# A four-layer graph network on one core: moved waits, moved exponentials, one moved matmul group and one moved scatter turn

## The reference, cut to what matters

```python
edge_index = jnp.stack([src, dst])
h = jnp.maximum(_layernorm(x, axis=-1), 0.0)
x = x + _L0_gnn_ref(h, ...)     # RGCN, 3 layers, 3 relations: relu(x[src] * (edge_attr @ nn_w.T + nn_b)), mean by (relation, dst), @ W[r]
h = jnp.maximum(_layernorm(x, axis=-1), 0.0)
x = x + _L1_gnn_ref(h, ...)     # gate = sigmoid(silu(rbf @ W1 + b1) @ W2 + b2); segment sum of gate * h[src]; update MLP
h = jnp.maximum(_layernorm(x, axis=-1), 0.0)
x = x + _L2_gnn_ref(h, ...)     # relational attention, below
h = jnp.maximum(_layernorm(x, axis=-1), 0.0)
x = x + _L3_gnn_ref(h, ...)     # distance attention, normalised by source node
```

```python
h_stack = jnp.einsum('ni,rdi->rnd', x, W)                 # 8 relations
h_src = h_stack[edge_type, src].reshape(-1, N_HEADS, HEAD_DIM)
h_dst = h_stack[edge_type, dst].reshape(-1, N_HEADS, HEAD_DIM)
attn = jax.nn.leaky_relu(sum(h_src * a_src) + sum(h_dst * a_dst), negative_slope=0.2)
attn = jax.nn.softmax(attn, axis=0)                       # over all edges
out = jax.ops.segment_sum(h_src * attn, dst, num_segments=num_nodes)
```

## Time and profile before

| what | us |
| --- | --- |
| median of 3 runs | 4981.04 |
| lowest and highest | 4974.59, 4981.15 |
| the profiled execution, its own time | 4983.89 |
| its span | 4982.0 |
| busy: PE, DVE, POOL, ACT | 3979.3, 3409.0, 3202.8, 1799.4 |

### The profile page before, as it was taken

One profiled execution on the slowest core, in us unless ns is written; L12 is line 12 of the kernel. 1 busy time (PEld: TensorE's weight loads), 2 busy tenths in 40 slices (PEclk: granted clock), 3 DMA queues, 4 the chain that ended last, 5 costly groups with the idle time before them and its releaser, 6 DMA issues. The chain is left out here.

```text
span 4982.0 us, 109658 instructions
## 1 busy us (share of the span) xinstructions
PE 3979.3 (80%) x22466; PEld 3275.0 (66%) x22467; DVE 3409.0 (68%) x9196; ACT 1799.4 (36%) x5526; POOL 3202.8 (64%) x3524
## 2 busy tenths in 40 slices
PE   6799996689987889878898466785967878578886
PEld 3477775677876778767787356674856667357665
DVE  7788886567756778577786667865237777755665
ACT  0454543121123333333332100012246667357774
POOL 0255554677756777667776677765677777247775
PEclk9799998899998999989999677897968888777787
DMA  1233333855525555264550787832454445234445
GB/s 45 91 120 120 117 120 98 196 143 153 161 61 172 147 145 159 58 191 136 149 160 21 229 246 218 243 101 82 144 101 107 102 102 105 57 97 108 108 109 99
DMA packets 633882, 637.83 MB, mean 128 GB/s; under 512 B 314926, under 2 KB 537460, under 8 KB 633716
## 3 DMA queue, kind: packets, MB, share of 16 engines
q0 software_dynamic: 149568, 384.54, 28.2%
q1 hardware_dynamic: 386164, 197.34, 14.6%
q10 hardware_dynamic: 97984, 54.35, 3.6%
HBM read 468.18 MB, written 166.84 MB: 127 GB/s over the span
## 5 line engine op out<-in xcount | busy, mean ns | idle before, releaser
L975 POOL DMA_INDIRECT G<-h_dram,idx x1572 | 1523.2, 969 | 534.8 <-issue 360.4
L1150 PEld LDWEIGHTS ps_a<-hotm,msg 128*128 128x128 f32 x4716 | 687.7, 194 | 202.1 <-DVE arena L1239 71.7
L1138 PE MATMUL ps_e<-nnw,attT 128*128 128x256 f32 x2358 | 736.1, 396 | 96.2 <-DVE prodm L1232 46.7
L1150 PE MATMUL ps_a<-hotm,msg 128*128 128x128 f32 x4716 | 729.4, 283 | 95.4 <-DVE arena L1239 93.0
L1239 DVE TENSOR_TENSOR arena<-ps_a,arena 128x256 f32 x1404 | 588.1, 419 | 214.3 <-issue 106.4
L770 POOL DMA_INDIRECT rec_dram<-rec,pos x392 | 378.7, 966 | 455.9 <-ACT rec L630 340.3
L975 POOL DMA_INDIRECT G<-feat_dram,idx x420 | 405.6, 966 | 266.9 <-POOLq L242 139.3
L1185 ACT ACTIVATE msg<-prodm 128x256 f32<-128x256 f32 x786 | 327.4, 417 | 669.4 <-DVE prodm L1232 597.0
L975 POOL DMA_INDIRECT arena<-rel_dram,idx x468 | 457.8, 978 | 158.4 <-issue 101.2
L792 POOL DMA_INDIRECT rec_dram<-now,to x396 | 391.2, 988 | 186.3 <-POOL to L789 103.4
L1138 PEld LDWEIGHTS ps_e<-nnw,attT 128*128 128x128 f32 x2358 | 368.2, 196 | 132.7 <-DVE prodm L1232 67.5
(11 more groups left out here) (349 smaller groups left out, 7953.2 us busy)
## 6 DMA issues: line engine op xcount, KB each, us to landing
gate<-rec_dram SPq DMA_DIRECT2D x126, 384.0 KB
G<-msg_dram SPq DMA_DIRECT2D x300, 128.0 KB
msg_dram<-msg ACTq DMA_DIRECT2D x270, 128.0 KB
rel_dram<-stage SPq DMA_DIRECT2D x25, 1040.0 KB
G<-h_dram,idx POOLq DMA_INDIRECT x1572
msg_dram<-arena ACTq DMA_DIRECT2D x90, 128.0 KB
at<-edge_attr SPq DMA_DIRECT2D x98, 112.0 KB
attT<-attT_dram SPq DMA_DIRECT2D x74, 144.0 KB
```

Of the source, the lines that this page charges most:

```text
L975: pool.indirect_dma_start(G[:, n % width, :], None, table, bass.IndirectOffsetOnAxis(ap=idx[:, which, n:n + 1], axis=0)).then_inc(sem(f"sw ...
L1138: t.matmul(ps_e[s % BANKS][:], attT[:, s // HU, s % HU, :], nnw[:], start=True, stop=True).then_inc(sem("ew"), 1)
L1150: last = t.matmul(ps_a[s % BANKS][:, h, :], of[:, h * P:(h + 1) * P], hot[:, s, :], start=True, stop=True)
```

## The change

Four edits:

1. In the sort's second block TensorE's first ranks (L677) go behind the second layer of the even step. Nothing else of the order changes.
2. In the relational pass ScalarE waits for `agg` in every fourth step instead of each step, and for `ad_e` in every second step; each wait covers the chunks up to the next one.
3. In the same pass ScalarE takes a group's two exponentials 14 steps behind its last chunk instead of 12.
4. Of the scatter by source, turn 39 goes into the gated update block. The three blocks that follow keep their number of turns or lose one: the normalisation has turns 40 to 42, the weights block 43 and 44, the rows block 45 to 65, one less than before.

```diff
@@ TensorE, sort's second block, in front of `if c2:`
-                            if c0:
-                                n, i, s = c0
-                                b = s // 2
-                                if s % 2 == 0:
-                                    pe.wait_ge(sem("hot"), i * 2 + b + 1)
-                                    for j in range(SG - 1):
-                                        last = t.matmul(ps_r[:, j + 1:SG, :], ..., start=False, stop=(j == SG - 2), ...)
-                                    last.then_inc(sem("before"), 1)
@@ behind it
-                                if s % 2 == 1:
+                                if s % 2 == 0:
+                                    pe.wait_ge(sem("hot"), i * 2 + b + 1)
+                                    ...
+                                    last.then_inc(sem("before"), 1)
+                                else:
                                     pe.wait_ge(sem("looked_up"), i * 2 + b + 1)
@@ scatter by source, four blocks
-                            scatter_by_source(pool, (33, 39))
+                            scatter_by_source(pool, (33, 40))
-        normalize(turns=(39, 42), early=[...])
+        normalize(turns=(40, 43), early=[...])
-                            scatter_by_source(pool, (42, 44))
+                            scatter_by_source(pool, (43, 45))
-                            scatter_by_source(pool, (44, EC2 // (G2 * GROUPS2)))
+                            scatter_by_source(pool, (45, EC2 // (G2 * GROUPS2)))
@@ ScalarE, relational pass
-                            for c0, c1, c2, c5, c12, c28 in walk(nc.scalar, TURNSR, 0, 1, 2, 5, 12, 28, ...):
+                            for c0, c1, c2, c5, c14, c28 in walk(nc.scalar, TURNSR, 0, 1, 2, 5, 14, 28, ...):
                                 if c1:
                                     n, i, s = c1
-                                    act.wait_ge(sem("agg"), upto(n - UR))
+                                    if s % 4 == 0:
+                                        act.wait_ge(sem("agg"), upto(n + 3 - UR))
                                     one_hot_row(act, c1, dist, hot[:, s, :])
                                 if c2:
                                     act.wait_ge(sem("hotT"), upto(n))
-                                    act.wait_ge(sem("ad_e"), upto(n - RING))
+                                    if s % 2 == 0:
+                                        act.wait_ge(sem("ad_e"), upto(n + 1 - RING))
-                                if ends_group(c12):
-                                    g, q, chunks = group(c12)
+                                if ends_group(c14):
+                                    g, q, chunks = group(c14)
                                     act.wait_ge(sem("fall"), upto(g))
```

More of the change, by code:

```diff
@@ L669, in _ @@
                                 last.then_inc(sem("z"), 1)
-                            if c0:
-                                n, i, s = c0
-                                b = s // 2
-                                if s % 2 == 0:
-                                    pe.wait_ge(sem("hot"), i * 2 + b + 1)
-                                    for j in range(SG - 1):
-                                        last = t.matmul(ps_r[:, j + 1:SG, :], identb[:], four(OK[:, b, j, :], SG - 1 - j),
-                                                        start=False, stop=(j == SG - 2), skip_group_check=True)
-                                    last.then_inc(sem("before"), 1)
                             if c2:
@@ L692, in _ @@
                                 b = s // 2
-                                if s % 2 == 1:
+                                if s % 2 == 0:
+                                    pe.wait_ge(sem("hot"), i * 2 + b + 1)
+                                    for j in range(SG - 1):
+                                        last = t.matmul(ps_r[:, j + 1:SG, :], identb[:], four(OK[:, b, j, :], SG - 1 - j),
+                                                        start=False, stop=(j == SG - 2), skip_group_check=True)
+                                    last.then_inc(sem("before"), 1)
+                                else:
                                     pe.wait_ge(sem("looked_up"), i * 2 + b + 1)
@@ L1755, in _ @@
                             credit(act, "dist", "hot", "hotT_sb", "ga", "fell", "w")
-                            for c0, c1, c2, c5, c12, c28 in walk(nc.scalar, TURNSR, 0, 1, 2, 5, 12, 28, width=UR, static=TURNSR - LASTT):
+                            for c0, c1, c2, c5, c14, c28 in walk(nc.scalar, TURNSR, 0, 1, 2, 5, 14, 28, width=UR, static=TURNSR - LASTT):
                                 if c28 and at_first_extra(c28):
@@ L1776, in _ @@
                                     nc.scalar.copy(picked[:, q, :, :, R8], G[:, q * GR:(q + 1) * GR, D:RW]).then_inc(sem("ga"), 1)
-                                if ends_group(c12):
-                                    g, q, chunks = group(c12)
+                                if ends_group(c14):
+                                    g, q, chunks = group(c14)
                                     act.wait_ge(sem("fall"), upto(g))
-                                    tiles_in = slice(0, TILES if extras_only(c12) else 1)
+                                    tiles_in = slice(0, TILES if extras_only(c14) else 1)
                                     nc.scalar.activation(fall[:, q, tiles_in, :], fall[:, q, tiles_in, :], ACT.Exp).then_inc(sem("fell"), 1)
@@ L2217, in build @@
         gated()
-        normalize(turns=(39, 42), early=[(W_in, L2_gnn_W.rearrange("r (h p) d -> p r h d", p=P))])
+        normalize(turns=(40, 43), early=[(W_in, L2_gnn_W.rearrange("r (h p) d -> p r h d", p=P))])
         relational_attention()
```

## The result

| what | before | after |
| --- | --- | --- |
| median, us | 4979.51 (4 runs beside it) | 4921.76 (4 runs, 4919.07 to 4924.07) |
| the profiled execution, its own time | 4983.89 | 4919.07 |
| its span | 4982.0 | 4917.2 |
| the sort's second block | 674.3 | 640.6 |
| relational rows block | 208.6 | 199.2 |

The ratio of after to before is 0.9886, 95% interval 0.9874 to 0.9898, a gain of 57.8 us; the prediction was 4928. The three blocks gained 33.7 + 9.4 + 12.3 = 55.4 of the 64.8 us between the two profiled executions. The rest lies in the other blocks, at most 3.5 us each. Two profiled executions differ by as much where nothing was changed: the pass took 2.8 us less than before in experiment 1, which leaves it alone.

What follows compares the result with a forecast made beforehand. TensorE, with holes, was taken to pace the sort's second block and GpSimd's gathers to cap the relational pass. 33 + 9.2 + 11 = 53 us off 4983.9 gave 4930.7, as a median 4928; range 4912 to 4958.

Steps and rivals of the forecast that it cites:

- Edit 1: Sort's second block: TensorE's holes waiting for VectorE's keys vanish, period 6.68 to 6.28 us; gain 33 us, between 24.9 and 39.
- The signs that it named: Sort's second block: L736's period near 6.3 us, no wait of L677 for the keys.
- The slack of VectorE's way round: Sort's loop from TensorE's first ranks through VectorE and back: 5.8 of 6.28 us, smallest spares about a third of a microsecond.
- Edit 4: Rows block loses a GpSimd scatter turn, hidden in the gated update's idle end: gain 9.2 us, at least 7, at most 9.5.
- Edits 2 and 3: Relational pass: ScalarE's stalls go, so gathers stop waiting for a full ring; gain 11 us, ends 4 (or 0) and 20.
- The gathers' pace: Relational pass: GpSimd's gathers can go every 1.25 us, 15.0 us per group of 12; the kernel before within 5% of that.
- if the stall stayed, only the fall wait would go, nearer 5 us: Relational pass: if ScalarE's 3.0 us stalls at loop jumps stayed, only its 2.0 us waits per group would go; sum nearer 5 us.
- I give them nothing by themselves: Relational pass: ScalarE's removed `agg` and `ad_e` waits stop nothing and only cost queue slots, so no gain of their own.
- The rule of the Trainium skill: ScalarE's relational loop: jumps outside two held blocks of 256 instructions stall for a fetch; a shorter body would lose the 3.0 us gaps.
- the smaller sort: Rival, sort's second block: a spare is gone, TensorE waits at L696 or L687, gain about 10 us, total 4951; chance 0.18.
- the slower case: Rival, sort's second block: the even silu gets between first ranks and VectorE's chain, total up to 5002 us; chance 0.03.
- Nothing from the relational part: Rival, relational pass: VectorE or TensorE's half clock fills the ring, not ScalarE, so no gain there, total 4939; chance 0.09.
- More: Rival: relational pass gains 20 us as its tail shrinks and engines run closer to the gathers, sort 39, total 4913; chance 0.05.

Runs made afterwards that it cites:

- experiment 1: The kernel before with only TensorE's first ranks moved behind the second layer: 4943.93 us against 4979.78, ratio 0.9934.
- experiment 5: The kernel before with only the scatter turn moved into the gated update: 4968.7 us against 4977.17, ratio 0.9981, median of eight of ten runs.
- experiment 2: The kernel before with only ScalarE's fewer `agg` and `ad_e` waits and exponentials at step 14: 4967.12 us, ratio 0.9976.
- experiment 3: The kernel before with only ScalarE's fewer `agg` and `ad_e` waits, exponentials kept at step 12: 4966.90 us, ratio 0.9974.
- experiment 4: The kernel before with only ScalarE's exponentials moved from step 12 to 14, all waits kept: 4967.91 us, ratio 0.9976.
- experiment 6: The kernel before with 64 already met waits (32 instructions) added to ScalarE's program before the relational loop, its body unchanged: 4964.14 us, ratio 0.9973.
- experiment 7: The changed kernel without the bias matmul of the gate MLP's second layer (L673): 4901.64 us, ratio 0.9846.

## Why the prediction was right, and where it was not

- **Edit 1** (33 us): 33.7 in the profile and 34.1 alone. The period added up from the starts was right within 0.03 us (6.28, measured 6.31). That 33 itself came so near is in part luck: it was the middle between 39 and 24.9, taken without a reason. The steady period fell by 0.37 us, which over 97 groups would be 36 us, and the first four groups, in which the loop fills, took 27.4 us where they had taken 27.6 and gave next to nothing. The signs that it named are all there. The slack of VectorE's way round, put at 5.8 us of 6.28, is borne out: 6.31 - 0.48 = 5.83.
- **Edit 4** (9.2 us): 9.4 and, alone, 9.7; the idle time in the gated update covered the turn, and the whole turn came off the rows block, where I had allowed for a store that ends it first. 9.5 was my upper end.
- **Edits 2 and 3** (11 us): 12.3. The sum was nearly right by two errors that cancelled, which is luck. The idle time of the full ring went as predicted: 153 us over all gathers before, 142 after (the waits of all 468). But the gathers themselves became longer, 461.5 / 468 = 0.986 us in the mean against 0.978, so that from first to last gather only 610.1 - 602.9 = 7.2 us were won. And the tail behind the last gather, which I had left as it was, became 5.1 us shorter: VectorE's last message starts 24.6 us behind the last gather (4236.3 and 4211.7) instead of 29.7. Part of that is scatter: in experiments 1 and 5, whose pass is unchanged, it is 26.7 and 29.0 us, and in experiments 2, 3, 4 and 6 it is 23.5 to 26.4.
- **The gathers' pace** was put at 1.25 us, with 1.25 to 1.28 as the sign of being right. It is (4211.7 - 3608.8) / 467 = 1.291. The 1.25 took the median gather of 0.946 us; with the mean of 0.978 that the prediction had too, the pace is 1.283 us and 15.4 us a group, so the kernel before, at 1.306, was within 2% of it and not 5%. For the same reason the upper end of this term should have been 11 + 0.03 x 468 = 25 us and not 20, and the low end is given as 4 and as 0. The chances of the four cases that were called faster add up to 0.94, where 0.93 is stated.
- **The step that failed** is the branch "if the stall stayed, only the fall wait would go, nearer 5 us". It treated the two stalls as two independent shares of the 11 us. Experiment 4 kept the jump stall and gained 11.9 us. What the step lacked is the pace that each stall alone would set: 44.4 us a turn with the falls, 41.1 at most with the jumps, against 46.0 for the gathers. The ring fills only with both, and either edit ends it. Likewise "I give them nothing by themselves" was right about the waits as waits and wrong about the edit: edit 2 alone gave 12.9 us, by the jump gaps that it ended (experiment 6 shows that these can be ended with every wait kept).
- **The rule of the Trainium skill** that I weighed gave the right change of the gap, and experiment 6 agrees with it, but whether it held made no difference to the time of this change: with edit 3 in, the kernel is as fast with the jump stall as without.
- **The rivals**: the smaller sort and the slower case needed a wait of L696 or L687 that has no row. "Nothing from the relational part" is refuted by experiments 2 to 4. "More" had the shrinking tail right, and the gathers' first-to-last time shrank by 7.2 us and no further.
- The parts add up: 35.9 + 12.7 + 8.4 (edit 4, the eight runs) = 57.0 us for the edits alone, 57.8 together.

No run here points to a version that beats the changed kernel with the whole reference kept: its sort is bound by TensorE's own order and its pass by the gathers.

## What to carry to other kernels

When a wait goes round in a loop over two engines, add up the starts of the fuller engine in its new order: that sum is the period to expect, and the spare of every loop through the other engine says whether it will hold. Don't share a gain out over two stalls that fill the same buffer: remove each alone, and ask what pace each would set without the present bound. Here a stall once per long loop body was caught up wherever the engine had slack, and one in every group was not.

## What the hardware showed that I had not expected

- A body of 287 instructions cost 3.0 us at each jump back, and 0.28 us once 32 instructions stood in front of it, with nothing in the body changed; that made the whole kernel 13 us faster.
- Leaving out a matmul that took 0.23 us of TensorE's order gained only 0.12 us, mostly since the eight matmuls behind it took 0.08 to 0.10 us longer.
- With idle time gone from GpSimd, the mean indirect gather of 128 rows became 0.008 us longer while the median stayed at 0.946: 71 of the 468 took over 1.0 us, 64 before. Over the other profiles with 468 gathers the mean is 0.977 and 0.981 us where the ring fills (experiments 5 and 1) and 0.978 to 0.992 where it doesn't (2, 3, 4, 6 and 7), so the two overlap; what makes a gather long stays open.
